# Small loads first on two queues, the adjacency held back, the last scalings on ScalarE: a change to a two-layer graph kernel

## The reference

```python
u = einsum('bnh,bmh->bnm', x, x) / sqrt(H);  scores = softmax(u)
delta = scores * adj;  att = delta / (sum(delta, 2) + 1e-10)
ctx = att_left @ (x @ Wl.T + bl) + att_self @ (x @ Ws.T + bs) + att_right @ (x @ Wr.T + br)
o = relu(ln_w * (ctx - mean) / sqrt(var + 1e-12) + ln_b)
x = layernorm(x + o)
d = (sum(adj, -1) + 1e-5) ** -0.5
x = layernorm(x + d[:, None] * adj @ (d[:, None] * x @ W1) + b1)
```

## Time and profile before

| | us |
|---|---|
| median of 3 runs (440.77 to 441.22) | 441.21 |
| the profiled execution, its time | 440.96 |
| its span, first to last instruction | 439.4 |
| PE busy in the span | 429.3 (98%) |
| DVE busy | 381.1 (87%) |
| ACT, POOL busy | 315.8, 302.6 |

### The profile page before, as it was taken

One profiled execution on the slowest core, in us unless ns is written; L12 is line 12 of the kernel. 1 busy time (PEld: TensorE's weight loads), 2 busy tenths in 40 slices (PEclk: granted clock), 3 DMA queues, 4 the chain that ended last, 5 costly groups with the idle time before them and its releaser, 6 DMA issues.

```text
span 439.4 us, 9038 instructions
## 1 busy us (share of the span) xinstructions
PE 429.3 (98%) x2761; PEld 353.6 (80%) x2761; DVE 381.1 (87%) x699; ACT 315.8 (72%) x660; POOL 302.6 (69%) x364
## 2 busy tenths in 40 slices
PE   7999999999999999999999999999999999999994
PEld 5689978779787888869887797977978789896753
DVE  2998999998999889997999989999799989998546
ACT  2689887868777787678876787676867777888420
POOL 2125666668776678758796687866877597797874
PEclk9999999999999999999999999999999999999998
DMA  5935878489665985478944888539866589244802
GB/s 160 357 98 137 265 183 240 155 200 262 141 191 137 265 231 144 146 176 274 226 138 116 213 272 213 161 99 217 285 152 189 135 229 300 60 110 108 191 25 73
DMA packets 68879, 79.90 MB, mean 182 GB/s; under 512 B 7232, under 2 KB 60608, under 8 KB 68832
## 3 DMA queue, kind: packets, MB, share of 16 engines
q1 hardware_dynamic: 68768, 79.26, 66.5%
q0 software_dynamic: 64, 0.07, 0.1%
HBM read 38.40 MB, written 4.19 MB: 97 GB/s over the span
## 4 chain that ended last, share of the span: by engine, by line
PE 95%; DMA 2%; DVE 1%; SPq 1%; issue 0%; ACT 0%; POOLq 0%; POOL 0%
PE ps_y L542 23%; PE ps_c L522 23%; PE ps_d L507 13%; PE ps_c L528 6%; PE ps_u L488 5%; PE ps_u L442 4%; PE ps_u L444 4%; PE ps_u L443 4%; PE ps_m L554 3%; PE ps_m L442 3%; PE ps_m L444 2%; PE ps_m L443 2%; DMA bias_bc<-in_L_gnn_bs_dram 2%; PE ps_u L542 1%; SPq L353 0%
## 5 line engine op out<-in xcount | busy, mean ns | idle before, releaser
L1487 POOL TENSOR_TENSOR dM<-dT,parts 128x384 f32<-128x384 f32 x64 | 72.0, 1126 | 64.1 <-ACT dT L860 52.1
L522 PE MATMUL ps_c<-h_sum,dT 128*128 128x128 f32 x896 | 110.4, 275 | 0.0
L522 PEld LDWEIGHTS ps_c<-h_sum,dT 128*128 128x128 f32 x896 | 106.4, 192 | 2.9 <-issue 2.5
L542 PE MATMUL ps_y<-aT,x1p 128*128 128x512 f32 x224 | 106.3, 593 | 0.0
L847 ACT ACTIVATE d_rows<-ps_u,nmax 128x1024 f32<-128x1024 f32 x62 | 68.8, 1109 | 50.2 <-DVE nmax L1130 50.2
L1130 DVE TENSOR_REDUCE nmax<-ps_u 128x1 f32<-128x1024 f32 x62 | 75.2, 1213 | 17.7 <-PE ps_u L488 15.9
L1137 DVE CUSTOM_DVE_ANT_0 d_rows<-d_rows,a_rows 128x1024 f32<-128x1024 f32 x64 | 84.2, 1323 | 0.3
L860 ACT ACTIVATE dT<-ps_d 128x1024 f32<-128x1024 f32 x64 | 65.3, 1020 | 25.7 <-PE ps_d L507 23.4
L1144 DVE STREAM_TRANSPOSE a_blk<-a_rows 128x1024 f32<-128x1024 f32 x64 | 77.7, 1228 | 0.0
L866 ACT ACTIVATE junk<-a_rows 128x1024 fp8e4<-128x1024 f32 x64 | 67.1, 1049 | 0.3
L507 PEld LDWEIGHTS ps_d<-parts,d_rows 128*128 128x128 f32 x512 | 58.9, 141 | 10.3 <-issue 9.5
(11 more groups left out here) (104 smaller groups left out, 743.7 us busy)
## 6 DMA issues: line engine op xcount, KB each, us to landing
a_rows<-in_adj_dram SPq DMA_DIRECT2D x64, 512.0 KB, 5.0
aT<-a_blk SPq DMA_DIRECT2D x224, 128.0 KB, 3.2
x_rows<-in_x_dram SPq DMA_DIRECT2D x8, 512.0 KB, 3.9
a_rows<-a_blk SPq DMA_DIRECT2D x32, 128.0 KB, 2.4
out_dram<-fin SPq DMA_DIRECT2D x15, 256.0 KB, 2.5
x_turned<-x_blk SPq DMA_DIRECT2D x96, 32.0 KB, 2.2
out_dram<-fin SPq DMA_DIRECT2D x1, 192.0 KB, 2.1
fin<-in_L_gnn_Wl_dram SPq DMA_DIRECT2D x1, 64.0 KB, 3.4
```

What stands on the lines that cost most here:

```text
L522: pe.matmul(ps_c[:, c_place(b, i), :], dT[:, i % 2, j, :], h_sum[:, b % 2, j, k * H:(k + 1) * H], start=t == 0, stop=False)
L542: last = pe.matmul(y_bank(b, i0, i1), gathered(b)[:, j, :], turned(b)[:, i0:i1, :, j, :].rearrange("p i q c -> p (i q) c"), start=j == 0, ...
L1487: pool.tensor_tensor(dM[:, i % 2, :, :], dT[:, i % 2, i, :].rearrange("p (a c) -> p a c", a=1).to_broadcast([P, 3, P]), parts[:, :, :], AL ...
```

## The change

It has five parts.

1. x of batch 0 comes in two halves with a semaphore each. PE turns both halves and then the weights, and the first `scores` need only what they read.
2. The biases, and the norm constants, are issued by POOL. The biases are now the very first thing on POOL, ahead of the identity. SP issues x and the weights and then waits until the biases have landed (`bias_in`) before the first adjacency strip.
3. In batch 0, `project` alternates between two banks, `ps_m` and `ps_y`.
4. At the end, `norm_f` for blocks 0 to 3 and 4 to 6 moves from DVE to ACT, which also issues the store of 4 to 6. Block 7 has no shift: DVE subtracts the mean and multiplies by the power.
5. All five lists are written out in a new order; every step is still there.

```diff
         def norm_f_on(eng, b, i0, i1):
-            eng.wait_ge(f_scale, NB * b + i1)
+            eng.wait_ge(f_scale if shifted(b, i1) else f_power, NB * b + i1)
             for i in range(i0, i1):
...
+                    last = eng.tensor_scalar(v, v, stats_last[:, 0, 1:2], by, ALU.subtract, ALU.mult)
...
+            def load_x_half(b, half):
+                sp.dma_start(x_rows[:, b, blocks_of(half), :], x_block_rows(x, b, HALF * half, HALF * (half + 1)))\
+                  .then_inc(x_in[b] if half else x0_in, 16)
...
             def load_weights():
                 for k, w in enumerate((Wl, Wr, Ws)):
                     sp.dma_start(wraw[:, k, :], w).then_inc(const_in, 16)
-
-            def load_biases():
-                for k, v in enumerate((bl, br, bs)):
-                    sp.dma_start(bias_bc[:, k * H:(k + 1) * H], v.partition_broadcast(P)).then_inc(bias_in, 16)
...
+                sp.wait_ge(bias_in, 48)
...
             def first_products():
                 pe.wait_ge(warm_in, 1)
-                for c in (slice(0, HALF), slice(HALF, HALF + 3 * P)):
-                    pe.matmul(ps_u[:, c], d_rows[:, 0, 0:P], d_rows[:, 0, 0:c.stop - c.start], start=True, stop=True)
+                zero = d_rows[:, 0, 0:P]
+                for n in (HB, 2):
...
+        def h_bank(b, j):
+            return (ps_y if b == 0 and j % 2 else ps_m)[:, 0:3 * H]
...
             def scores(b, i):
                 g = NB * b + i
-                pe.wait_ge(xt_split, 2 * (b + 1))
+                if b or i >= HB:
+                    pe.wait_ge(xt_split, 2 * (b + 1))
...
+                    if b == 0 and i < HB:
+                        pe.wait_ge(xt_split, 2 if c.start else 1)
...
-            pe.wait_ge(const_gp, 6)
+            pe.wait_ge(const_gp, 2)
...
+            def norm_f(b, i0, i1):
+                act.wait_ge(f_scale, NB * b + i1)
+                act.wait_ge(f_norm, NB * b + i0)
+                normalize(fin, fin, "f", i0, i1).then_inc(f_norm, i1 - i0)
...
             def constants():
-                pool.memset(parts[:, 0:2, :], 1.0).then_inc(const_gp, 1)
-                pool.memset(parts[:, 2, :], 0.0).then_inc(const_gp, 1)
-                pool.memset(minus_half[:, :], -0.5).then_inc(const_gp, 1)
-                pool.wait_ge(const_gp, 3)
+                for k, v in enumerate((bl, br, bs)):
+                    pool.dma_start(bias_bc[:, k * H:(k + 1) * H], v.partition_broadcast(P)).then_inc(bias_in, 16)
+                pool.memset(ident, 0.0).then_inc(const_gp, 1)
+                pool.wait_ge(const_gp, 1)
                 pool.affine_select(out=ident, in_=ident, compare_op=ALU.not_equal, fill=1.0,
                                    base=0, pattern=[[-1, P]], channel_multiplier=1).then_inc(const_gp, 1)
```

More of the change, by code:

```diff
@@ L669, in batch @@
-                scores(b, 0)
                 m_read_o(p - 1, 0, HB)
@@ L1046, in last_batches @@
                 keep(b, 1)
+                diagonal(p, 6)
                 d_out(b, 0)
@@ L1057, in last_batches @@
                 keep(b, 3)
-                degree(b, 2)
+                d_out(b, 2)
+                diagonal(b, 0)
                 degree(b, 3)
                 diagonal(b, 1)
-                d_out(b, 2)
                 exps(b, 4)
@@ L1275, in first_batches @@
-                row_sums(p, 0)
-                turn_blocks(p, 1)
                 turn_blocks(p, 2)
                 row_max(p, 6)
+                x_low(b, 1)
                 masked(p, 5)
                 turn_blocks(p, 3)
+                row_max(p, 7)
+                row_sums(p, 0)
+                masked(p, 6)
+                turn_blocks(p, 4)
+                add_self(p, 0, HB)
+                row_max(b, 0)
+                stats_c(p, 0, HB)
+                add_bias(b, 0)
+                masked(p, 7)
@@ new lines, in first_batches @@
+                turn_blocks(p, 5)
+                add_bias(b, 1)
+                row_max(b, 1)
+                turn_blocks(p, 6)
+                add_bias(b, 2)
+                turn_blocks(p, 7)
+                stats_x(p, 0, HB)
+                masked(b, 0)
+                row_max(b, 2)
+                row_sums(p, 1)
+                add_bias(b, 3)
+                add_self(p, HB, NB)
+                stats_c(p, HB, NB)
+                add_bias(b, 4)
+                masked(b, 1)
+                add_bias(b, 5)
@@ new lines, in first_batches, with batch @@
+                row_max(b, 3)
+                masked(b, 2)
+                add_bias(b, 6)
+                turn_blocks(b, 0)
+                add_bias(b, 7)
+                turn_blocks(b, 1)
+                row_max(b, 4)
+                stats_x(p, HB, NB)
+                turn_blocks(b, 2)
+                masked(b, 3)
+                row_max(b, 5)
+                turn_rows(b)
+                turn_blocks(b, 3)
+                turn_blocks(b, 4)
+            def batch(b, p):
+                masked(p, 4)
+                masked(p, 5)
+                row_max(p, 6)
+                turn_blocks(p, 5)
+                add_out(p - 1, 0, HB)
+                row_sums(p, 0)
+                stats_f(p - 1, 0, HB)
+                turn_blocks(p, 6)
```

764 lines of the change are left out of this document (364 added, 400 removed).

## The result

The changed kernel takes **443.55 us** (median of 6 runs, 442.25 to 443.88), the kernel before 440.9 in the same comparison: a ratio of 1.0052, with a 95% interval of 1.0034 to 1.0070. It is slower by about 2.3 us, where 437.4 was forecast. The profiled execution took 442.89 us with a span of 441.1, against 440.96 and 439.4 before, so 1.7 us of span have to be found.

The account below looks back on a forecast made before the run. PE was taken to bound the middle, DVE to set the start's pace. Start 3.2 plus end 0.6, middle zero, made 3.8 us: span 439.4 to 435.6, profiled 437.2, median 437.4 (own range 436.4 to 438.4; wider 435.9 to 439.9).

Parts of the forecast that it names:

- Identity and x: Start: three bias issues cost POOL 2.7 us, identity ready at 4.3 (3.6 to 5.5), PE turns x at 4.4.
- It now goes out one issue later (0.44), lands at about 6.1.: Start: third weight matrix, taking 3.3 us as before, is turned by about 6.5; scores start at 6.9 to 7.0.
- DVE's list from there to the first context product: Start: from the first row maximum at 8.5, DVE needs 14.4 us plus 0.2; context product at 23.2.
- The rule that I cited against the hold: Queues share 16 engines, so a second saves only issue time; biases would keep 7.0 us, making the sum 1.4 worse, 438.8.
- rival 2: Start: PE's clock rises later because first_products has less to do; row maxima 1.5 us later, 438.9; chance 0.07.
- The hold: Start: SP's wait for biases is hidden with 1.1 us to spare, first strip at 10.9; at 7.0 landing it costs 1.4.
- I cost the new orders at zero; their cover is that spare time.: Middle: new orders cost nothing, since DVE has 4.6 us of 52 to spare, ACT 12.8, POOL 13.5.
- Rival 3: Middle: POOL's rows_with_bias waits for a store, delaying PE five times; with 1.0 us each the time is 442.4; chance 0.08.
- The end: End: last scaling 0.6 us earlier (0 to 1.1), as DVE loses scalings and a shift but POOL is 0.4 late.
- The gain of the start: Start: first context product at 23.2 instead of 26.38, 3.2 us gained (2.1 to 3.7).
- Rival 1: Start: slow bias issues and late bias landing bite; start gains 1.0, time 439.6, with half of it 438.8; chance 0.18.

Follow-up runs that it names:

- e1: Changed kernel with the three biases on SP behind the weights and norm constants on SP behind a batch 1 strip, hold kept: 440.36 us, ratio 0.9988.
- e2: Changed kernel with the weights turned behind the first block of scores, on PE and DVE, loads unchanged: 442.05 us, ratio 1.0031.
- e7: Changed kernel with its six small loads reading 128 different weight rows instead of one broadcast row (wrong values, same work): 439.45 us, ratio 0.9953.
- e9: e6 with the three biases issued as ACT's first instructions, beside x, without SP's hold: 444.31 us, ratio 1.0074.
- e13: e9 with the three bias loads reading 128 different weight rows instead of one broadcast row (wrong values): 439.60 us, ratio 0.9975.
- e6: e5 without SP's wait for the biases before the strips: 438.0 us, ratio 0.9920, the fastest version with all of the reference's work.
- e4: Kernel before with the new end (part 4) alone: 440.55 us, ratio 0.9997.
- e5: e1's head with its hold and the new end, but the kernel before's orders from batch 0's last block of scores on: 438.93 us, ratio 0.9941.
- e8: Changed kernel without SP's wait for the biases before the strips: 444.57 us, ratio 1.0072.
- e12: e1 with context_near(p, 3) moved behind the last gather in batch, five times: 446.56 us, ratio 1.0125.
- e11: e6 with the end of the kernel before (scalings and store on DVE and SP, block 7 with its shift): 438.32 us, ratio 0.9944.

## Why the prediction was wrong

The span was to be 435.6 and was 441.1. The 5.5 us fall to three places: the first context product 3.5 late (26.70 for 23.2), the middle 1.5, the end 0.5. The median is 0.66 above the profiled time and not 0.25, and the profiled time 1.8 above the span and not 1.6, which makes up the rest to 6.15.

- **Identity and x.** Right in the mechanism. Three bias issues took 1.9 us of POOL (at 1.32, 2.10 and 2.65) for the 2.7 I took, and PE turned x at 4.05, within the bounds of 3.6 to 5.5, but earlier than the 4.2 to 4.6 that I named as a sign.
- **"It now goes out one issue later (0.44), lands at about 6.1."** This is the step that failed. I took the 3.3 us of the earlier trace rows for the weights as theirs, while the change put three broadcasts beside them. They landed at 8.3. That is 1.6 us on the start of `scores`, and through the idle PE it brought the lower clock, another 1.3 on the first row maximum. DVE's list from there to the first context product took 15.2 us for the 14.7 that I took (11.47 to 26.70), the last 0.5. e1 takes the wait and the low clock away, e2 too for the first row maximum but not the late strips, e7 shows the cause. I had weighed the biases' landing only for the hold, not for what they do to others; the same had a bias at 7.0 us, and I read it as a delay that it suffers.
- **The rule that I cited against the hold** (the Trainium skill, DMA: Bandwidth & Descriptors, Issuing engines are not separate DMA queues) was right in a way that I had not applied. e9 and e13 agree with it: loads on ACT's queue delay x on SP's (5.6 and 4.0 us, for 3.0 in e6). The rule speaks of shared engines; that a broadcast row costs its neighbours far more than its bytes is in the runs.
- **The clock.** It was rival 2 in part, by another way: not the shorter `first_products`, as e1 shows, but a fall after the 2.6 us that PE stood idle. The Trainium skill, TensorE: Matmul & The Clock Gate (What's actually happening), says that the rise varies from run to run. The traces agree, by more than I had allowed for: 6.5 us before and 13.3 in e4, with 2.5 us on the first context product.
- **The hold.** It was hidden, but by luck. The last bias took 5.3 us to land, between the 4.4 and the 7.0, and the first strip 6.5 more and not 3.8, so it landed at 14.4 for the 10.9 of the forecast. With `scores` on time `masked` would have wanted it at 12.0. In the changed kernel it wanted it at 15.3; in e2, with `scores` early, it waits 1.28 us. With plain rows (e7) the strip takes 3.6. The hold's price, 0 in the forecast, is 0.9 in e5 and about -1.0 in the changed kernel's place (e8).
- **"I cost the new orders at zero; their cover is that spare time."** The second step that failed, 1.5 us. The spare time of DVE, ACT and POOL over 52 us is no cover: what counts is whether each copy is ready when PE comes to it, and after this reordering ACT's `yT` comes 0.07 us late, with nothing on PE to cover it. e5 shows that the orders do it. Rival 3 named another place (POOL's `rows_with_bias` behind a store); no wait for it is seen. The gaps at `second_product`, seven times 0.15 us, are 1.0 of the 1.5, those in `gather` 0.3; the last 0.2 stays open, and so does a remedy: the one that was aimed at them (e12) closed them and broke another chain.
- **The end.** Mis-sized: 0.6 forecast, 0.1 in the changed kernel, 0.3 in e4 and in e11 against e6, where POOL's order is the old one. POOL was late as forecast; what I left out is that the store issued by ACT stands behind its own last scaling, and takes 0.5 longer to the end of the span.
- **The gain of the start.** 3.2 us were there to be had: e7 has its first context product at 23.17, where 23.2 was forecast for the changed kernel. So the sum of the start was right but for the landing of the weights and what hangs on it.
- **Rival 1.** Half of its loss of 2.2 us gives 438.5 and not 438.8.

## What to carry to other kernels

A small load is not small by its bytes. One row broadcast to 128 partitions, issued beside urgent loads, delayed them by 2 us and more from either of two other queues; behind them on the same queue it cost nothing. So put broadcasts in time, behind what is urgent, and ask of every moved load what it does to its neighbours' landing, not only when it lands itself.

On an engine that is full, an order can't be costed by the spare time of the others. Look for each copy that it reads, and by how much that is ready early; a move of half a us in a loop run five times cost 6 us, and waits too short for the chain of waits to show cost some 1.3 in all.

A part of a change should be run alone before the whole: here the new head, with its loads in SP's order and no hold, is worth 2.6 us with the old middle and the old end (e11), and the new orders of the middle alone take 1.4 back (e1 against e5).

## What the runs showed of the hardware

- A broadcast bias on POOL's queue is made of 16 packets of 4096 bytes of up to 2.65 us each (plain rows there, e7: up to 0.53); on SP's and ACT's queues of 128 packets of 512 bytes, mostly of 0.027 us. Both forms delay others. Why the second does is not seen in its packets: in e9 the engines moved 87, 120 and 175 GB/s in the three slices from 1.9 to 3.8 us, in e13, with plain rows, 98, 182 and 322. This stays open.
- In the changed kernel PE's clock fell from 2.4 to 1.2 GHz when work came back after 2.6 us of idling early in the run (5.7 to 8.3), and stayed there from 8.7 to 12.1. With an idle time of 1.6 us at about the same place (e6, 5.3 to 6.9) it did not fall; in e9, with two idle times of 1.6 and 1.4 us (4.0 to 5.7 and 6.3 to 7.7), it did, at 7.9.
- The time at which the clock first rises is not fixed by the program: about 6.5 us in the trace before, 13.3 in that of e4, which has the same instructions there. The column of the granted clock shows 1.00 for that stretch of e4 all the same; before the first rise only the distance between matmuls tells it.
